# Gated linear attention with a quantized feed-forward network on eight cores: copies moved from the vector engine to the scalar engine, and output stores of two chunks joined

## The reference

```python
x = L0_attn_x                                     # (4, 4096, 1024)
# attention, 8 heads of 128
q = l2norm(x @ Wq); k = l2norm(x @ Wk); v = x @ Wv
alpha = sigmoid(x @ Wg)
def step(S, qkva):
    S = a_t[..., None] * S + k_t[..., None] * v_t[:, :, None, :]
    o_t = einsum('bhkv,bhk->bhv', S, q_t)
x = layernorm(x + o @ Wo)
# feed-forward: both products with activations rounded to 8 bits and weights to -1, 0, 1
h = gelu(bitlinear(x, w1, b1))
x = layernorm(x + bitlinear(h, w2, b2))
```

## Time and profile before

| | us |
|---|---|
| median of 2 runs | 3915.47 (3914.15 to 3916.79) |
| profiled execution | 3911.46 |
| its span on the slowest core (core 6) | 3909.9 |
| spans of the 8 cores | 3894.7 to 3909.9 |
| up to the first window chunk (0 to 491) | 491 |
| heads, from the first window chunk to the last (491 to 1666) | 1175 |
| projection stage (1735 to 2412) | 677 |
| feed-forward stage (2495 to 3909) | 1414 |

### The profile page before, as it was taken

How to read it: one execution, slowest core, us unless ns; L and a number is a source line. 1 busy time by engine, 2 the same in 40 slices (tenths; PEclk the granted TensorE clock), 3 DMA queues, 4 the chain that set the end, 5 groups by cost and what they waited for, 6 DMA issues and landing times.

```text
span 3909.9 us, 26926 instructions; the slowest of 8 cores (3894.7 to 3909.9 us)
## 1 busy us (share of the span) xinstructions
PE 1355.4 (35%) x5666; PEld 629.1 (16%) x5750; DVE 1608.0 (41%) x3442; ACT 628.4 (16%) x1352; POOL 209.2 (5%) x408
## 2 busy tenths in 40 slices
PE   5444343433533434311111111433333333344433
PEld 2111121211211211200000000111111111211111
DVE  0233233333333334334554444444445555444444
ACT  1100222222222222200000000111111111111111
POOL 0000111021011110200000000000000000000000
PEclk9766655656555555555555555776666666667766
DMA  4101110102102102042222222000000000000000
GB/s 71 38 27 30 30 43 25 52 16 61 53 15 61 42 26 52 17 132 70 73 74 80 79 80 67 11 11 11 11 11 11 11 11 11 11 11 11 11 11 16
DMA packets 162864, 145.27 MB, mean 37 GB/s; under 512 B 108048, under 2 KB 124560, under 8 KB 161552
## 3 DMA queue, kind: packets, MB, share of 16 engines
q1 hardware_dynamic: 139344, 123.88, 10.8%
q0 software_dynamic: 23360, 19.66, 3.5%
HBM read 129.61 MB, written 29.36 MB: 41 GB/s over the span
## 4 chain that ended last, share of the span: by engine, by line
DVE 35%; PE 27%; DMA 14%; issue 11%; ACT 9%; POOL 2%; DVEq 1%; SPq 1%; ACTq 0%; POOLq 0%; another core or an unknown queue 0%
PE ps L822 6%; PE ps L455 3%; DMA wsl<-wg 3%; DVE u1b L739 2%; PE ps L620 2%; DVE bigb L397 2%; PE ps L274 2%; ACT lneg L744 2%; DMA lneg<-w2t 2%; DVE u1b L801 2%; DVE wsl L805 2%; DVE sct L751 2%; DVE remz L793 2%; DMA lneg<-w1t 2%; DMA wsl<-od 2%
## 5 line engine op out<-in xcount | busy, mean ns | idle before, releaser
L733 PE MATMUL ps<-bigb,wsl 128*128 128x512 bf16 x1008 | 254.6, 417 | 194.7 <-DMA wsl<-n1scr 193.8
L811 PE MATMUL pt<-c_iden,wsl 128*128 128x128 bf16 x512 | 59.8, 308 | 709.0 <-DVE wsl L805 707.5
L503 DVE SCALAR_TENSOR_TENSOR ssb<-ps,ssb 128x128 f32<-128x128 f32 x288 | 84.1, 292 | 493.6 <-PE ps L455 299.1
L822 PE MATMUL ps<-biga,wsl 128*128 128x512 bf16 x992 | 247.7, 413 | 22.0 <-DVE wsl L816 21.2
L455 PE MATMUL ps<-c_idenf,yf 128*128 128x128 f32 x288 | 135.7, 471 | 283.0 <-POOL yf L452 282.8
L620 PE MATMUL ps<-wsl 128*128 128x512 bf16 x248 | 86.9, 521 | 342.6 <-DMA wsl<-od 341.7
L739 DVE SCALAR_TENSOR_TENSOR u1b<-ps,scp,cuml 128x512 f32<-128x512 f32 x128 | 96.1, 751 | 260.3 <-PE ps L733 131.3
L477 PE MATMUL ps<-amsk,biga 64*128 64x64 bf16 x256 | 53.3, 208 | 337.5 <-DVE amsk L472 337.5
L811 PEld LDWEIGHTS pt<-c_iden,wsl 128*128 128x128 bf16 x512 | 50.8, 140 | 721.7 <-issue 720.2
L733 PEld LDWEIGHTS ps<-bigb,wsl 128*128 128x128 bf16 x1024 | 106.5, 105 | 342.6 <-issue 243.8
L837 ACT ACTIVATE u1b<-yf 128x1024 f32<-128x1024 f32 x16 | 16.9, 1056 | 847.3 <-DVE yf L833 847.3
(11 more groups left out here) (158 smaller groups left out, 2762.8 us busy)
## 6 DMA issues: line engine op xcount, KB each, us to landing
lneg<-w1t SPq DMA_DIRECT2D x64, 256.0 KB, 2.9
lneg<-w2t SPq DMA_DIRECT2D x64, 256.0 KB, 3.0
qscr<-biga SPq DMA_DIRECT2D x32, 256.0 KB, 2.3
lneg<-w1t SPq DMA_DIRECT2D x4, 2048.0 KB, 9.7
cuml<-w1t SPq DMA_DIRECT2D x4, 2048.0 KB, 14.4
lneg<-w2t SPq DMA_DIRECT2D x4, 2048.0 KB, 8.2
cuml<-w2t SPq DMA_DIRECT2D x4, 2048.0 KB, 13.9
u1b<-xtm SPq DMA_DIRECT2D x16, 512.0 KB, 4.8
```

What stands on the lines that cost most here:

```text
L503: q.scalar_tensor_tensor(ssb[:, nxt * 128:nxt * 128 + 128], psO[:, 64:192], 1.0, ssb[:, cur * 128:cur * 128 + 128], ALU.bypass, ALU.add),
L733: mms = [(lambda q, c=c, s=s, bank=bank, n1a=n1a: q.matmul(ps[bank][:, 0:512], n1a[:, c * 128:(c + 1) * 128], t1q[:, c * 4096 + s * 512:c ...
L811: trs = [(lambda q, cb=bb * 8 + kk, kk=kk, pv=pv: q.transpose(pv[:, kk * 128:(kk + 1) * 128], N2TM[:, cb * 128:(cb + 1) * 128], c_iden[:]) ...
L822: mms.append(lambda q, c2=c2, half=half: q.matmul(ps[4 + half][:, 0:512], N2F[:, c2 * 128:(c2 + 1) * 128], t2q[:, c2 * 1024 + half * 512:c ...
```

## The change

- The copy of the state to bf16 goes from DVE (L463) to ACT (`activation` with Copy).
- The two halves of ostg are now filled by two successive window chunks, and one store of 128 columns follows the second, where there was a store of 64 columns per chunk. The state update names the matching half.
- The copy out of pt6 in the projection stage (L707) and the four copies per tile out of pt6 and pt7 in the feed-forward stage (L816) go from DVE to ACT.
- Two constants that nothing read are no longer set.

```diff
--- before.py
+++ after.py
@@ -191,7 +191,7 @@
         c_idenf = e(nc.sbuf_tensor("c_idenf", [128, 128], F32))
         c_tri = e(nc.sbuf_tensor("c_tri", [128, C], BF16))
         c_ones = e(nc.sbuf_tensor("c_ones", [128, 1], BF16))
-        cstv = e(nc.sbuf_tensor("cstv", [128, 5], F32))
+        cstv = e(nc.sbuf_tensor("cstv", [128, 3], F32))
 
         ps = [e(nc.psum_tensor(f"ps{i}", [128, 512], F32)) for i in range(6)]
         pt6 = e(nc.psum_tensor("pt6", [128, 1024], BF16))
@@ -238,8 +238,6 @@
         P.emit("DVE", lambda q: q.memset(cstv[:, 0:1], 1e-5), writes=["cstv"])
         P.emit("DVE", lambda q: q.memset(cstv[:, 1:2], 1.0 / D), writes=["cstv"])
         P.emit("DVE", lambda q: q.memset(cstv[:, 2:3], 1.0 / FF), writes=["cstv"])
-        P.emit("DVE", lambda q: q.memset(cstv[:, 3:4], -0.5), writes=["cstv"])
-        P.emit("DVE", lambda q: q.memset(cstv[:, 4:5], 0.5), writes=["cstv"])
         P.dma("SP", "consts", c_iden[:], diden[:], ["d_iden"], ["c_iden"], k=4)
         P.dma("SP", "consts", c_idenf[:], didenf[:], ["d_idenf"], ["c_idenf"], k=4)
         P.dma("SP", "consts", c_tri[:], dtri[:], ["d_tri"], ["c_tri"], k=4)
@@ -460,8 +458,9 @@
                     AF.Copy, bias=0.0, scale=rk_c),
                     reads=[kK, "rk"], writes=[f"khts{par}"])
                 if ci >= NCP:
-                    P.emit("DVE", lambda q, cur=cur: q.tensor_copy(
-                        sbf[:], ssb[:, cur * 128:cur * 128 + 128]),
+                    P.emit("ACT", lambda q, cur=cur: q.activation(
+                        sbf[:], ssb[:, cur * 128:cur * 128 + 128],
+                        AF.Copy, bias=0.0, scale=1.0),
                         reads=[f"S{cur}"], writes=["Sbf"])
                     P.emit("PE", lambda q, sl=sl, q_sl=q_sl, psS=psS, row0=row0,
                            tp=tp: q.matmul(
@@ -485,15 +484,20 @@
                             v_c, start=True, stop=True),
                     ], reads=[f"amsk{par}", "vt", "Sbf", "qhb", f"khts{par}"],
                         writes=[kO])
-                    P.emit("ACT", lambda q, psO=psO, par=par: q.activation(
-                        ostg[:, par * 64:par * 64 + 64], psO[:, 0:64],
+                    wc = ci - NCP
+                    osl = wc % 2
+                    P.emit("ACT", lambda q, psO=psO, osl=osl: q.activation(
+                        ostg[:, osl * 64:osl * 64 + 64], psO[:, 0:64],
                         AF.Copy, bias=0.0, scale=1.0),
-                        reads=[kO], writes=[f"ostg{par}"])
-                    tloc = (ci - NCP) * C
-                    P.dma("SP", "ostore",
-                          d_o[h8 * 128:(h8 + 1) * 128, tloc:tloc + C],
-                          ostg[:, par * 64:par * 64 + 64],
-                          [f"ostg{par}"], ["d_o"], k=4)
+                        reads=[kO], writes=[f"ostg{osl}"])
+                    if osl == 1 or ci == NCA - 1:
+                        tloc = (wc - osl) * C
+                        P.dma("SP", "ostore",
+                              d_o[h8 * 128:(h8 + 1) * 128,
+                                  tloc:tloc + (osl + 1) * C],
+                              ostg[:, 0:(osl + 1) * 64],
+                              [f"ostg{k}" for k in range(osl + 1)],
+                              ["d_o"], k=4)
                 else:
                     P.emit("PE", lambda q, psO=psO, row0=row0, v_c=v_c: q.matmul(
                         psO[:, 64:192], khts[row0:row0 + 64, 0:128],
@@ -505,7 +509,7 @@
                            ssb[:, cur * 128:cur * 128 + 128],
                            ALU.bypass, ALU.add),
                        reads=[f"S{cur}", kO] +
-                             ([f"ostg{par}"] if ci >= NCP else []),
+                             ([f"ostg{(ci - NCP) % 2}"] if ci >= NCP else []),
                        writes=[f"S{nxt}"])
                 P.emit("DVE", lambda q, ci=ci, nxt=nxt: q.tensor_scalar(
                     ssb[:, nxt * 128:nxt * 128 + 128],
@@ -704,8 +708,9 @@
                 pt6[:, cb * 128:(cb + 1) * 128], N1S[:, cb * 128:(cb + 1) * 128],
                 c_iden[:])) for cb in range(8)]
             P.group("PE", trs, reads=["n1tm", "c_iden"], writes=["pt6"])
-            P.emit("DVE", lambda q: q.tensor_copy(N1S[:, 1024:2048], pt6[:]),
-                   reads=["pt6"], writes=["n1st"])
+            P.emit("ACT", lambda q: q.activation(
+                N1S[:, 1024:2048], pt6[:], AF.Copy, bias=0.0, scale=1.0),
+                reads=["pt6"], writes=["n1st"])
             P.dma("SP", "n1store",
                   d_n1scr.rearrange("(c t p) n -> t p c n", c=DC, p=128)
                   [t, :, :, :],
@@ -813,8 +818,9 @@
                     N2TM[:, cb * 128:(cb + 1) * 128], c_iden[:]))
                     for kk in range(8)]
                 P.group("PE", trs, reads=["n2tm", "c_iden"], writes=[pk])
-                P.emit("DVE", lambda q, bb=bb, pv=pv: q.tensor_copy(
-                    N2F[:, bb * 1024:(bb + 1) * 1024], pv[:]),
+                P.emit("ACT", lambda q, bb=bb, pv=pv: q.activation(
+                    N2F[:, bb * 1024:(bb + 1) * 1024], pv[:],
+                    AF.Copy, bias=0.0, scale=1.0),
                     reads=[pk], writes=["n2F"])
             mms = []
             for c2 in range(FC):
```

## The result

The changed kernel takes 3930.7 us in the median (11 runs, 3923.7 to 3936.9), the kernel before 3917.7 us (10 runs). The ratio is 1.0032, 95% interval 1.0022 to 1.0042: about 13 us slower, inside the 2% either way. The forecast was 3939 us in a range of 3886 to 3966, and +23.6 us. The direction, the place of each term and the cancelling in the recurrence were right; the loss was forecast nearly twice too large.

The account below looks back on a forecast made before the run. A chain going from engine to engine, not any engine's busy time, was taken as the bound. Terms -2.6 + 5.9 + 20.3 = +23.6 us on the profiled 3911.5, with the median 4.0 above, gave 3939 us, range 3886 to 3966.

Parts of the forecast that it names:

- What bounds: Whole kernel: a chain from engine to engine sets the time; an instruction counts only if it stands in that chain.
- The recurrence: 256 window chunks: moving the state copy saves 20.5 us, added wait at the update loses 17.9; net 2.6 us gained.
- the two prices: Waits behind the last to come: about 0.07 us more at DVE's update; PE starts 0.25 us behind ACT, not 0.14.
- The one-price rival: Waits in recurrence and feed-forward stage cost the same whatever their number: -26.2 us in all, 3889 us; chance 0.14.
- The paired store: One store for two window chunks: half as many stores, costed at nothing, with a few us for rare long landings.
- The cover: Paired store: 2.16 us from issue to the next eviction needing that half, against a median landing of 1.4.
- the rival: Paired store's landing enters the turn at each pair's first eviction; beyond 2% from 2.8 us landings; chance 0.05.
- The projection stage: Copy out of pt6, 16 tiles: ACT takes 0.37 us longer, all on the path, 5.9 us lost.
- The feed-forward stage: Four copies per tile on ACT: 4.78 us for 3.51, 1.27 more in each of 16 tiles, 20.3 us lost.

Follow-up runs that it names:

- e10: Kernel before, with the state update also waiting for DVE's own, long satisfied semaphore between ACT's and PE's: ratio 1.0045, +18 us.
- e11: Kernel before, with the two waits of PE's group in a window chunk turned to DVE, then ACT: ratio 1.0077, +30 us.
- e1: Kernel before, with only the state copy moved from DVE to ACT: ratio 0.9990 (0.9980 to 1.0001), -4 us.
- e6: Kernel before, with the state update's two waits turned to PE, then ACT: ratio 0.9957, -17 us.
- e8: Kernel before, with the waits of the feed-forward stage's bias instruction turned to DVE, PE, ACT (7 of 8 per tile): ratio 0.9944, -22 us.
- e5: Changed kernel, with ACT's wait put last at PE's group and the state update: 3873.8 us, ratio 0.9888 to the kernel before.
- e9: Kernel before plus state copy on ACT, paired stores, ACT's wait last at update, PE's group and feed-forward bias; PSUM copies on DVE: 3832.7 us, ratio 0.9791.
- e4: Kernel before, with only the projection stage's copy moved from DVE to ACT: ratio 1.0011 (0.9999 to 1.0023), +4 us.
- e3: Kernel before, with only the feed-forward stage's four copies per tile moved from DVE to ACT: ratio 1.0033, +13 us.
- e7: Kernel before, with state copy on ACT and ACT's wait last at PE's group and the state update: ratio 0.9852, -58 us.

## Why the forecast held, and where it missed

- **What bounds**: right. The chain from engine to engine decided; 113.7 us taken from DVE's busy time bought nothing where DVE was not what came last.
- **The recurrence** (-2.6 us): right as a sum and by its parts. DVE to ACT 0.10 was forecast and stands in the row; the copy 0.30, measured 0.309; ACT to PE 0.25, measured 0.25; the update 0.24, measured 0.24. The turn is 2.517 us against 2.522 in the mean of eight cores: -1.3 us in 256. The time from the first state copy to the last can't resolve that, since in one kernel it differs between the cores by more (1161.5 to 1175.3 us before). e10 and e11 test the two prices by themselves.
- **The one-price rival** (waits cost the same whatever their number): wrong. Its -49 us for the recurrence is excluded by e1, and e6, e8, e10 and e11 each move only the list of waits and move the time. It is the place and not the number alone that counts: three waits with the last to come at the end start 0.10 us behind it (e8), as one does. The Trainium skill's Perfetto Trace Analysis, "DVE / Act Engine Instruction", has an instruction wait until all semaphores are satisfied and gives no price by their number or order. These programs put each wait into the queue by itself, ahead of the instruction, and their delays on DVE were 0.10, 0.18 and 0.24 us with none, one and two waits behind the last to come. Why such a wait costs time was not tested.
- **The paired store** (nothing): right. The cover was forecast at 2.16 us, and from a store's issue to the next eviction it is 2.19 in the median. The landings were nearly all shorter: at a turn of 2.49 us one to five evictions per core waited for a store, at 2.27 (e5, e9) two to seven. So the point at which the rival would decide was never reached, and no run tests it.
- **The projection stage** (+5.9): right in kind, slightly too large; 1.023 us for 1.056 makes it 0.33 x 16 = 5.3, and e4 has +4, with an interval from 0 to 9.
- **The feed-forward stage** (+20.3): mis-sized; e3 has +13. The step that failed is "after: each copy 1.06, and each but the first waits ... (two waits, 0.18 as at L503): 4 x 1.06 + 3 x 0.18 = 4.78". The row of the changed kernel:

```profile
3059.28 4.53 ACT L821 ACTIVATE wsl<-pt 128x1024 bf16<-128x1024 bf16 x4 [29.98 <-PE pt L816]
```

  4.53 (4.55 in the mean of 16 tiles), so 1.02 to 1.04 more than before and not 1.27: the copy is 1.023 (I took the row of a Square from SBUF with an accumulator), and the gap between two is (4.53 - 4 x 1.023) / 3 = 0.15, not DVE's 0.18. A further part came from a place that the change doesn't touch, the short instructions between the sums and the quantization. One tile before:

```profile
3019.06 0.16 DVE L770 TENSOR_TENSOR sct<-sct 128x1 f32<-128x1 f32 x1
3019.52 0.15 DVE L773 TENSOR_SCALAR sct<-sct 128x1 f32<-128x1 f32 x1 [0.30 <-DVE sct L770]
```

  and in the changed kernel the same two:

```profile
3029.66 0.16 DVE L775 TENSOR_TENSOR sct<-sct 128x1 f32<-128x1 f32 x1
3029.93 0.15 DVE L778 TENSOR_SCALAR sct<-sct 128x1 f32<-128x1 f32 x1
```

  They are 0.46 apart in the one and 0.27 in the other. From L759 to L787 it is 4.17 us in the mean of 14 tiles before and 3.90 after; e3 has 3.92, e8 4.17 and e9, with the copies on DVE again, 4.15. But e4, whose feed-forward stage is untouched, has 3.89. So the gap goes with what was queued earlier in the program, not with the copies alone. Nor does it belong to L773: before, nearly every tile has one such delay between L759 and L787, of about 0.19 and 0.35 us in turn, and after every second tile it stands one instruction later (core 6, 15 of 16 tiles; here it is ahead of L773, two tiles later behind it). That fits a delay that comes at a fixed distance in DVE's queue; its cause stays open. Not all of it is gained, since some shows up in the quantization behind it: from L787 to the first copy it is 28.28 us before, 28.36 in the changed kernel and 28.43 in e4. In sum 1.04 - 0.27 + 0.08 - 0.06 (the second product, 16.12 us against 16.18) = 0.79 us per tile, the 0.79 by which a tile grew; 16 tiles make 12.6 us, and e3 has +13.

Of the whole error, 23.6 against 13, the feed-forward term is about 7 us. The rest, the projection's 2 among it, is of a size that these runs can't resolve. In the recurrence the total is no luck, since the two prices that cancel were each right.

## What to carry to other kernels

Before moving an instruction to an idler engine, work out what comes last at its consumer, and count the waits that will stand behind that one: here 0.07 us on DVE and 0.11 us on PE, together 0.18 us per turn, nearly all of the 0.19 that the move would have saved without them (0.73 to 0.54 us from the state to PE). Put the semaphore that comes last at the end of the list; alone, without any other edit, this was worth 17 us (update) and 22 us (bias; some 13 of them by the order itself, the others came with PE's clock, as told below). The state copy's move, worth 4 us by itself, came to 58 us together with the waits in order. A copy on the path between two engines that both wait for it belongs on the engine that does it soonest, 0.69 against 1.02 us here, however idle the other is.

## What the runs showed of the hardware that was not expected

- The same 64 products of the second layer take two different times, by what PE's clock does. In the kernel before they end about 16.2 us behind the last copy in every tile (core 6). In one of these tiles the clock is granted at half, 1.2 GHz, as they begin:

```profile
3053.00:3054.00 1.00, 1.00 (x3) 0.36 (x3) 0.00 (x0) 0.00 (x0) 0.00 (x0) 0.50 0.00 0
3054.00:3056.00 2.00, 2.00 (x6) 0.68 (x5) 0.00 (x0) 0.00 (x0) 0.00 (x0) 0.50 0.00 0
3056.00:3058.00 2.00, 2.00 (x10) 0.83 (x9) 0.00 (x0) 0.00 (x0) 0.00 (x0) 0.86 0.00 0
```

  (stretch, its length, busy us of PE, PEld, DVE, ACT and POOL, granted clock, DMA share, GB/s; the products start at about 3052.5.) In e8_before_order_ff, core 6, seven of 16 tiles take 14.2 us, the others 16.3 to 16.6, nearly in turn. In a short one the clock is at its upper level, 2.4 GHz, from the first product on:

```profile
3047.00:3048.00 1.00, 0.03 (x1) 0.06 (x2) 0.69 (x1) 0.00 (x0) 0.00 (x0) 1.00 0.00 0
3048.00:3049.00 1.00, 1.00 (x5) 0.45 (x6) 0.00 (x0) 0.00 (x0) 0.00 (x0) 1.00 0.00 0
```

  Ahead of them PE did the same 32 transposes and the same 3.5 us of copies ran on DVE, and PE had stood idle before the transposes, here for 43.3 us. But here the clock rose while the transposes still ran (at 3046.3 us), where in the kernel before it rose four microseconds into the products (at 3056.5). The work differed only in the tile's length, by the 0.8 us of the order. The mean is 15.5 against 16.2 us, 0.7 us per tile or 11 us in all on that core, enough to account for e8's gain beyond the 13 us of the bias stretch (16 x 0.83). Other cores of the kernel before have a few such tiles too (three of 16 on cores 4 and 5). In the changed kernel the products take 15.5 to 17.2 us, but in the mean of eight cores 16.1 against 16.0 before, so this accounts for at most 2 us of its 13. What decides in which tile the clock rises early was not tested.
- The turn of the recurrence alternated between 2.43 and 2.57 us in the kernel before, by the 0.14 or 0.26 us between the starts of the copy L463 and the mask behind it. With the copy on ACT both sorts of chunk have 2.49, because ACT, not the mask, is the last to come. The mask still starts at two distances (0.18 or 0.06 us ahead of the copy), and once PE's waits are in order the later one shows again, as 2.27 for 2.25 us (e5, e7). The cause of the alternation was not tried.
